# Perceiver block on one core: first transfers issued in turn with a fixed first chunk, and another order around the gate and the first expert block

## The reference

```python
x = x + xattn(layernorm(x), ctx, ctx, mask)     # 16 batches x 64 queries, 1601 keys, 16 heads of 32
x = x + attn(layernorm(x))                      # self-attention of 64 tokens, q and v with a LoRA term
x = x + ffn(layernorm(x))                       # 20 experts, top 2 of a softmax gate
...
scores = jnp.where(mask == 0, NEG, scores)      # one mask for all batches
...
h = gelu(xf @ wg1 + bg1); probs = softmax(h @ wg2 + bg2)[:, :20]
top_vals, top_idx = lax.top_k(probs, 2)
y = sum over experts of g_e * (xf @ We_e + be_e)
```

## Time and profile before

| | us |
|---|---|
| median of 3 executions | 780.59 |
| lowest, highest | 780.42, 781.32 |
| the profiled execution's own time | 780.74 |
| its span in the trace | 778.9 |
| TensorE busy | 707.7 (91%) |
| VectorE busy | 409.8 (53%) |
| ScalarE busy | 360.5 (46%) |
| GpSimd busy | 283.1 (36%) |
| mean granted TensorE clock | 0.962 |

### The profile page before, as it was taken

One profiled execution on the slowest core, in us unless ns is written; L12 is line 12 of the kernel. 1 busy time (PEld: TensorE's weight loads), 2 busy tenths in 40 slices (PEclk: granted clock), 3 DMA queues, 4 the chain that ended last, 5 costly groups with the idle time before them and its releaser, 6 DMA issues.

```text
span 778.9 us, 16989 instructions
## 1 busy us (share of the span) xinstructions
PE 707.7 (91%) x6829; PEld 582.2 (75%) x6829; DVE 409.8 (53%) x937; ACT 360.5 (46%) x664; POOL 283.1 (36%) x259
## 2 busy tenths in 40 slices
PE   0899999999999999999999999999999856999970
PEld 0697888879887888788788877887778653688860
DVE  4833334454344334533553345725377547699965
ACT  1425344544454345435453343534456331499950
POOL 0004155414542354235532453522225132666530
PEclk9999999999999999999999999999999975799995
DMA  9401101211121001100110002020001682699918
GB/s 289 150 1 43 44 2 43 98 38 62 43 98 44 18 27 43 44 16 30 44 44 2 3 3 74 8 107 10 3 29 57 232 308 98 211 372 388 340 53 323
DMA packets 30779, 74.77 MB, mean 96 GB/s; under 512 B 4052, under 2 KB 5076, under 8 KB 29666
## 3 DMA queue, kind: packets, MB, share of 16 engines
q1 hardware_dynamic: 26290, 65.16, 23.7%
q0 software_dynamic: 4400, 8.41, 3.1%
HBM read 66.13 MB, written 13.44 MB: 102 GB/s over the span
## 4 chain that ended last, share of the span: by engine, by line
PE 84%; DVE 6%; issue 4%; DMA 2%; ACT 2%; POOL 0%; SPq 0%; POOLq 0%; DVEq 0%; ACTq 0%
PE bank L187 22%; PE bank L189 20%; PE bank L188 20%; PE bank L193 11%; PE bank L346 4%; PE bank L323 3%; DVE x_sb L1602 1%; DMA xi<-scratch_xn,tok 1%; DMA wr<-scratch_ys 1%; PE bank L561 1%; PE bank L548 1%; PE bank L577 1%; DVE wh L1076 1%; DVE stats L1330 0%; ACT wh L754 0%
## 5 line engine op out<-in xcount | busy, mean ns | idle before, releaser
L1628 POOL TENSOR_SCALAR pp<-pp,rl 128x400 f32<-128x400 f32 x128 | 163.8, 1297 | 234.8 <-DVE rl L1173 234.8
L1228 DVE COPY pt<-bank 128x512 f32<-128x512 f32 x64 | 44.3, 692 | 99.4 <-PE bank L193 99.3
L187 PE MATMUL bank<-chi,wk 128*128 128x400 f32 x256 | 93.5, 365 | 0.0
L837 ACT ACTIVATE pp<-pp,acc 128x400 f32<-128x400 f32 x128 | 79.0, 619 | 28.0 <-DVE acc L1261 27.7
L1261 DVE CUSTOM_DVE_ANT_0 pp<-bank,cap 128x400 f32<-128x400 f32 x128 | 66.8, 569 | 46.5 <-PE bank L323 46.5
L189 PE MATMUL bank<-chi,wk 128*128 128x400 f32 x256 | 88.3, 345 | 0.0
L188 PE MATMUL bank<-clo,wk 128*128 128x400 f32 x256 | 88.3, 345 | 0.0
L187 PE MATMUL bank<-wv,chi 128*128 128x512 f32 x200 | 83.5, 417 | 0.0
L189 PE MATMUL bank<-wv,clo 128*128 128x512 f32 x200 | 78.5, 392 | 0.0
L188 PE MATMUL bank<-wv,chi 128*128 128x512 f32 x200 | 78.5, 392 | 0.0
L754 ACT ACTIVATE pt<-bank 128x512 f32<-128x512 f32 x64 | 38.2, 597 | 76.4 <-PE bank L193 75.3
(11 more groups left out here) (236 smaller groups left out, 1388.4 us busy)
## 6 DMA issues: line engine op xcount, KB each, us to landing
wr<-in_We SPq DMA_DIRECT2D x13, 1024.0 KB, 12.3
craw<-in_ctx SPq DMA_DIRECT2D x16, 800.0 KB, 4.3
raw<-in_We SPq DMA_DIRECT2D x8, 1024.0 KB, 9.1
acc<-in_We SPq DMA_DIRECT2D x6, 1024.0 KB, 9.6
scratch_xn<-acc SPq DMA_DIRECT2D x16, 256.0 KB
wr<-scratch_ys SPq DMA_DIRECT2D x8, 512.0 KB, 7.9
x_sb<-in_x SPq DMA_DIRECT2D x2, 1024.0 KB, 11.5
out_dram<-x_sb SPq DMA_DIRECT2D x8, 256.0 KB, 5.2
```

The lines of the kernel that those rows point to most:

```text
L187: pe.matmul(o, lhs[0], rhs[0], start=start, stop=False)
L837: act.activation(frame(p8), frame(p8), ACT.Exp, bias=bias, scale=-1.0, accum_out=total).then_inc(S["a_exp"], 1)
L1228: dve.tensor_copy(pt[:, p8 % 4, :, :].rearrange("p a c -> p (a c)"), at("t", 8 * (n - 1) + p8)[:, :]).then_inc(S["v_pt"], 1)
L1628: pool.tensor_scalar(frame(p8), frame(p8), rl[:, n % 2, p8:p8 + 1], None, ALU.mult).then_inc(S["g_pn"], 1)
```

## The change

It has two parts. In the first, the chunks are laid out in reverse in memory, so that the last 400 keys are chunk 0, and chunk 0 is always the first to be done; its context and mask are loaded without waiting for `ids`, which only decide on further chunks. The flags come from a second copy of the mask (`rows`), laid out in rows of 8,000 bytes. SP issues constants, lora, x, rows; waits for the constants and issues wq; waits for x and issues the context; waits for the mask and issues wk and the second half of x. VectorE takes all four statistics of x ahead of the mask, and works out `ids` behind the low half of wk (`used`); the small transposes and products for it are moved in TensorE's order too.

In the second, a Gelu on one column is run in step 9, Gelu of the first gate half stands in step 12 ahead of the copy of tile 7, the gate product of the first half is one pass of 512 columns, that of the second half is cut in two of 256 columns of which the first stands behind the turn of tile 6. The splits of expert weight 1 are moved, the high half behind the second Gelu, the low half into block 0 with that of weight 2. All biases stand ahead of the first turn of tokens. Weights 6 and 7 wait for gather 1 too, and go out ahead of weight 9.

```diff
@@ tensor
-            pe.wait_ge(S["v_ids"], 2)
-            pe.matmul(pb[7][0:1, 0:10], fr[:, :], cst[0:NC_, 128:138], start=True, stop=True).then_inc(S["p_ids"], 1)
...
-            for i in range(4):
-                turn_x(i)
+            turn_x(0)
+            turn_x(1)
+            pe.wait_ge(S["v_ids"], 2)
+            pe.matmul(pb[7][0:1, 0:10], fr[:, :], cst[0:NC_, 128:138], start=True, stop=True).then_inc(S["p_ids"], 1)
+            turn_x(2)
+            turn_x(3)
...
+                elif what == "ga":
+                    pe.wait_ge(S["v_n2"], 14)
+                    pe.wait_ge(*before("g1", 1))
+                    gate_part(1, slice(0, 256))
                 else:
-                    pe.wait_ge(S["v_g1"], 1)
-                    pe.wait_ge(S["v_n2"], 8 + 4 * i + 3)
-                    pe.wait_ge(*before("g1", i))
-                    for c in (slice(0, 384), slice(384, 512)):
...
+                    pe.wait_ge(S["v_n2"], 12 + 4 * i)
+                    if i == 0:
+                        pe.wait_ge(S["v_g1"], 1)
+                        pe.wait_ge(*before("g1", 0))
+                    gate_part(i, slice(256 * i, 512)).then_inc(S["p_g1"], 1)
+
+            def gate_part(i, c):
+                for k in range(4):
+                    last = mm3(pe, pb[bank_of("g1", i)][:, c], [w[:, k, :] for w in g1],
+                               [v[:, k, i * 512 + c.start:i * 512 + c.stop] for v in xu], k == 0, k == 3)
+                return last
...
-            biases(range(3, 6))
+            biases(range(3, 8))
             turn_tokens(0)
-            biases(range(6, 8))
@@ beside
-                  ([("pj", 6)], [], [("n2", 5)]), ([("pj", 7)], [], [("g1", 0), ("n2", 6)]),
+                  ([("pj", 6)], [], [("n2", 5)]), ([("pj", 7)], [], [("g1", 0), ("n2", 6), ("ga", 1)]),
@@ scalar
                 if step >= 8:
                     norms(step)
+                if step == 9:
+                    act.activation(warm[:, :], gw[:, 20:21], ACT.Gelu)
+                if step == 12:
+                    gelu(0)
...
-                if step == 11:
-                    we_hi(1)
-                if step == 12:
-                    gelu(0)
             gelu(1)
+            we_hi(1)
@@ vector
-            dve.wait_ge(S["d_cap"], 32)
...
+            def used():
...
+            dve.memset(fl[:, 0:1], 1.0)
+            dve.wait_ge(d_x[0], 16)
+            for i in range(4):
+                own.on(bn(i))
             variance(0, 4)
+
+            dve.wait_ge(S["d_cap"], 32)
+            dve.tensor_reduce(cm[:, :], mska, AX.X, ALU.max, apply_absolute_value=True).then_inc(S["v_cap"], 1)
...
+            dve.tensor_scalar(fl[:, 1:NC_], cm[:, 1:NC_], rows[:, 2:3], None, ALU.max).then_inc(S["v_ids"], 1)
             scaled(0, 4)
             apply_x(0)
             apply_x(1)
             weight_lo(wh[0], raw[:, 0], 1)
+            dve.wait_ge(S["p_ids"], 1)
+            dve.tensor_reduce(fr[:, :], pb[7][0:NC_, 0:128], AX.X, ALU.max).then_inc(S["v_ids"], 1)
             for i in range(4):
                 turn_x(i)
                 if i < 2:
                     apply_x(i + 2)
+                elif i == 2:
+                    dve.wait_ge(S["p_ids"], 2)
+                    dve.tensor_copy(frow[:, 0:10], pb[7][0:1, 0:10]).then_inc(S["v_ids"], 1)
             context(0)
             weight_lo(wk, raw[:, 1], 2)
+            dve.wait_ge(S["v_ids"], 3)
+            used()
             dve.wait_ge(d_x[1], 16)
...
-            we_lo(1)
-
...
-            biases(range(6))
+            biases(range(8))
...
             def block_of(n):
                 turn_tokens(n + 1)
+                if n == 0:
+                    we_lo(1)
+                    we_lo(2)
...
             turn_tokens(0)
-            biases(range(6, 8))
-            we_lo(2)
@@ sync
             sp.dma_start(cst[:, :], t["cst"]).then_inc(S["d_cst"], 16)
-            for h in range(2):
-                sp.dma_start(mska[64 * h:64 * h + 64, :, :], t["mask"].rearrange("c q k -> q c k")).then_inc(S["d_cap"], 16)
+            sp.dma_start(lora[:, :, :], t["lora"]).then_inc(S["d_par"], 16)
             xv = t["x"].rearrange("(i b) q d -> i (b q) d", b=2)
             sp.dma_start(x_sb[:, 0:4, :], xv[0:4].rearrange("i p d -> p i d")).then_inc(d_x[0], 16)
+            for h in range(2):
+                sp.dma_start(mska[64 * h:64 * h + 64, :, :], t["rows"]).then_inc(S["d_cap"], 16)
+            sp.wait_ge(S["d_cst"], 16)
             sp.dma_start(raw[:, 0], t["wq"]).then_inc(d_raw[0], 16)
+            sp.wait_ge(d_x[0], 16)
+            sp.dma_start(craw[:, :, :], t["ctx"][0, 0]).then_inc(S["d_ctx"], 16)
+            sp.wait_ge(S["d_cap"], 32)
+            sp.dma_start(raw[:, 1], t["wk"]).then_inc(d_raw[1], 16)
             sp.dma_start(x_sb[:, 4:8, :], xv[4:8].rearrange("i p d -> p i d")).then_inc(d_x[1], 16)
-            sp.dma_start(raw[:, 1], t["wk"]).then_inc(d_raw[1], 16)
-            sp.dma_start(lora[:, :, :], t["lora"]).then_inc(S["d_par"], 16)
...
-            chunk = chunk_of(0)
-            context(0, 0, chunk)
-            load_cap(chunk, 0)
+            for h in range(2):
+                sp.dma_start(mski[64 * h:64 * h + 64], t["mask"][0]).then_inc(S["d_cap"], 16)
+            sp.dma_start(excl[:, :], t["excl"][0]).then_inc(S["d_cap"], 16)
             sp.wait_ge(S["v_w"], 1)
             sp.dma_start(raw[:, 0], t["wv"]).then_inc(d_raw[0], 16)
...
                 elif n < R:
                     sp.wait_ge(S["p_tab"], 1)
+                    sp.wait_ge(d_xi[1], 16)
...
-            for n in (R, R + 1, 6, 7, R + 2):
+            for n in (R, 6, 7, R + 1, R + 2):
                 load_weight(n)
@@ arrays
-        "ctx": ctx.reshape(16, NC, CW, 4, 128).transpose(0, 1, 4, 3, 2),
-        "mask": mask.reshape(64, NC, CW).transpose(1, 0, 2),
+        "ctx": ctx.reshape(16, NC, CW, 4, 128)[:, ::-1].transpose(0, 1, 4, 3, 2),
+        "mask": mask.reshape(64, NC, CW)[:, ::-1].transpose(1, 0, 2),
+        "rows": mask.reshape(64, NC, CW)[:, ::-1],
```

More of the change, by code:

```diff
@@ L126, in perceiver @@
         gmg = sb("gmg", [128, 2, 8])
+        warm = sb("warm", [128, 1])
         rb = sb("rb", [128, 2, 16])
@@ L714, in perceiver @@
         place = [(("wl", k), 4 + k) for k in range(4)] + [(use, n % 3) for n, use in enumerate(ring)]
-        dense_uses = [use for step in beside for part in step for use in part if use[0] != "n2"]
+        dense_uses = [use for step in beside for part in step for use in part if use[0] not in ("n2", "ga")]
         place += [(use, n % 2) for n, use in enumerate(dense_uses)]
@@ L1101, in vector @@
[L1101 to L1116, removed]
-                dve.wait_ge(own.sem, own.n)
-                own.on(dve.scalar_tensor_tensor(out=frow[:, 15:20], in0=frow[:, 5:10], scalar=float(j + 1),
-                                                in1=frow[:, 10:15], op0=ALU.is_equal, op1=ALU.mult,
-                                                accum_out=frow[:, 20 + j:21 + j]))
@@ L1121, in vector @@
-            dve.wait_ge(own.sem, own.n)
-            dve.tensor_copy(ids[:, 0:5], frow[:, 20:25]).then_inc(S["v_ids"], 1)
-            dve.tensor_copy(ids[:, 5:6], frow[:, 9:10]).then_inc(S["v_ids"], 1)
+            def used():
+                own.on(dve.tensor_tensor(frow[:, 10:15], frow[:, 0:5], cst[0:1, 142:147], ALU.mult))
+                for j in range(NC_):
+                    dve.wait_ge(own.sem, own.n)
+                    own.on(dve.scalar_tensor_tensor(out=frow[:, 15:20], in0=frow[:, 5:10], scalar=float(j + 1),
+                                                    in1=frow[:, 10:15], op0=ALU.is_equal, op1=ALU.mult,
+                                                    accum_out=frow[:, 20 + j:21 + j]))
+                dve.wait_ge(own.sem, own.n)
+                dve.tensor_copy(ids[:, 0:5], frow[:, 20:25]).then_inc(S["v_ids"], 1)
+                dve.tensor_copy(ids[:, 5:6], frow[:, 9:10]).then_inc(S["v_ids"], 1)
@@ L1272, in cross @@
                     share(n, 3, seg)
-            own.on(bn(2))
-            own.on(bn(3))
+            dve.memset(fl[:, 0:1], 1.0)
+            dve.wait_ge(d_x[0], 16)
+            for i in range(4):
+                own.on(bn(i))
             variance(0, 4)
+            dve.wait_ge(S["d_cap"], 32)
+            dve.tensor_reduce(cm[:, :], mska, AX.X, ALU.max, apply_absolute_value=True).then_inc(S["v_cap"], 1)
+            dve.wait_ge(S["v_cap"], 1)
+            own.on(dve.tensor_scalar(cm[:, :], cm[:, :], 0.0, None, ALU.not_equal))
+            dve.wait_ge(own.sem, own.n)
+            own.on(dve.tensor_reduce(rows[:, 0:1], cm[:, :], AX.X, ALU.max))
+            dve.wait_ge(own.sem, own.n)
+            dve.tensor_scalar(rows[:, 1:2], rows[:, 0:1], SCALE, None, ALU.mult)
+            own.on(dve.tensor_scalar(rows[:, 2:3], rows[:, 0:1], -1.0, 1.0, ALU.mult, ALU.add))
+            dve.wait_ge(own.sem, own.n)
+            dve.tensor_scalar(fl[:, 1:NC_], cm[:, 1:NC_], rows[:, 2:3], None, ALU.max).then_inc(S["v_ids"], 1)
```

(4 more changed lines are left out.)

27 lines of the change are left out of this document (8 added, 19 removed).

## The result

The changed kernel takes 773.37 us (median of four runs, 771.37 to 774.41) beside 780.96 for the kernel before on the same chip: ratio 0.9904, 95% interval 0.9885 to 0.9922. A second set of five runs gave 773.86 and 0.9912 [0.9898, 0.9926]. So it is faster, by about 1%, clear of the noise: 7.6 us where 11.1 were forecast. The profiled execution took 774.41 us, span 772.6, mean granted clock 0.960 (before 0.962).

What follows compares the result with a forecast made beforehand. TensorE was taken as the bound, so only the start and the holes between projection and first expert block could shrink: 780.74 - 5.3 - 2.5 - 3.3 = 769.6 us, range 766.6 to 773.4.

Steps and rivals of the forecast that it cites:

- Part 1: Start of the kernel: earlier x and reordered issues bring the first query matmul 5.3 us earlier, bounds 2.4 to 5.7.
- x at 6.6: Start: the first half of x, issued at about 1.7, lands 4.9 us later, at 6.6 us; high bound 9.65.
- 8,000-byte rows ... if it lands like x ... at 9.3: Start: the mask, in 8,000-byte instead of 1,600-byte rows, lands about 2.7 us behind x, at 9.3.
- wq follows at 12.0: Start: wq lands at 12.0 behind the mask; landing at 14.67 as before would leave 3.2 us of the gain.
- first statistic after 9: Start: sign that would show the forecast wrong; the first statistics of x were expected near 6.6 us.
- x shares the engines: Rival, start: wq, rows and x in flight together, x near 8.6 to 9.6, gain 2.4 to 3.2, total 772.1; chance 0.17.
- short rows: Start: argument against the shared-engines rival, that the mask's 1 MB needed to 9.65 before because its rows were short.
- Part 2: Gate: warm-up Gelu, split gate product and moved weight copy bring the second Gelu 2.5 us earlier, bounds 0.5 to 4.4.
- (b): Gate: moving ScalarE's weight 1 copy and splitting the gate product put the second Gelu at 632.0, not 634.87.
- (a): Gate: the warm-up Gelu's table load at step 9 widens the hole ahead of tile 5 from 2.4 to 3.9, +1.5 us.
- Part 3: First expert blocks: biases, not gather 0, bind; first turn 5.1, block 0 7.7 behind the gather, not 11.0; 3.3 earlier.
- 3.9 us of backlog: Expert blocks: delayed weight loads leave 1.5 MB behind, cutting the last weight's lead from 4.7 to 0.7; price 0, at most 2.

Runs made afterwards that it cites:

- wq_first: Changed kernel with wq issued ahead of the two mask row transfers; one execution, 774.32 us beside 782.62 for the kernel before.
- start_only: Kernel before with only the start of the change (issues, rows, order of VectorE's first steps); 779.33 us against 781.25, ratio 0.9976.
- gate_only: Kernel before with only the gate and first-block changes, its start unchanged; 775.89 us, ratio 0.9934 to the kernel before.
- bias_banks: Changed kernel with the gate and expert bias products in a ring of five banks instead of three; 772.35 us, ratio 0.9893 to the kernel before.
- rows128: Changed kernel with mask rows laid out for 128 partitions and loaded in one transfer instead of two to 64; one execution, 773.33 us.
- mask_fifth: Changed kernel with one of five mask chunks loaded for the flags and reduced, 0.2 MB instead of 1.0; one execution, 767.68 us.

## Why the prediction was partly wrong

**Part 1 failed:** it gave 2.7 us at the first query matmul instead of 5.3, and this alone moves the 769.6 of the forecast to 772.2. The step was "x at 6.6", with "8,000-byte rows ... if it lands like x ... at 9.3" and "wq follows at 12.0". Measured: 9.0, 12.7 and 15.2. The prediction had named a first statistic after 9 as a sign that it was wrong; it came at 9.01. The reason given, that the order of landing is the order of issue, is true (wq_first), but order is not speed. Of the 2.4 us by which x was late 0.8 is x alone (5.7, where the 4.9 of wv was taken over) and 1.6 the company; and the rows, though their lines were five times longer, moved at 224 to 230 GB/s and held wq as well. The working behind the landings was right: with the rows at 12.73 put into it the scaling stands 3.1 us earlier and the first query matmul 2.7, as measured, and with one transfer to 128 partitions that matmul comes at 22.7.

The rival "x shares the engines" had the size (2.4 to 3.2 us; 2.7 measured at the first matmul), and gave 772.1. Its mechanism is half of it: beside wq x was hardly later than alone, beside the rows it was. It rested on the mask before, which had needed to 9.65, and the prediction put that aside as "short rows"; the 211 to 221 GB/s of before, at a share of 1.06 to 1.07, were there to be read, and rows five times longer did not raise them.

**A term was missing:** the clock outside the gate. The pause at 482 costs 1.3 us when the clock falls behind it, and whether it falls changes from kernel to kernel with shifts of what comes ahead. It was put at nothing, and so was the slow stretch behind the first query matmul, which happened to be 6 matmuls shorter in after's profiled run: 1.1 us in the forecast's favour, by luck, since start_only, with the same start, had 13 slow ones. The prediction looked for slow clocks only where the rows of before showed one, in the gate.

**Part 2 was right in every event** (hole 3.9, no load beside the Gelu, no second load, 21.7 to the gather), and its size depends on the clock: (b) was costed with 4.6 us from the turn of tile 5 to the end of the projection, as in before (4.66) and in gate_only (4.59); in the profiled run it took 5.95, with 0.43 a matmul throughout. From turn 5 to the second Gelu 3.0 us were saved in the profiled run, and 4.4 in gate_only; less the 1.5 of (a), that is 1.5 and 2.9, where 2.9 had been worked out and 2.5 taken (13.2 us from turn to Gelu had been worked out, 13.21 were measured in gate_only). The Trainium skill (ScalarE: Activation LUTs, What ACT_TABLE_LOAD costs) adds a drain of 1.38 us to each switch; the load began 0.02 us behind the norm, took 1.28, and its activation began 0.02 behind it, so the trace does not agree. The same page (Table sets: the hidden batching unit) says that copy and identity are in every set, and there the trace agrees: between 610 and 630.67 copies, identities and two Gelus ran without a load.

**Part 3 was right** in its cause and its two distances, 5.1 and 7.7, and bias_banks confirms that the biases bind. Of the 3.3 us 2.2 are left at token tile 3, because block 0 and the turn behind it ran at 1.2 GHz to the end (5.25 us for 12 matmuls and 1.05 for the turn). The lead of the weights never showed: landings of 15.7 at worst, 4.1 us of lead at the last weight, the same 81.24 us, so the 3.9 us of backlog were a pessimistic sum.

In the profiled runs 6.3 us stand for the 11.1 forecast. The 4.8 are: 2.6 at the first query matmul, less 1.3 that came back up to 487 (1.1 of it the fewer slow matmuls behind the first query matmul), 1.3 at the pause of 482, 1.0 in the gate, 1.1 at block 0, and 0.1 behind the last scatter. The medians, 7.6 apart, hold less of the clock's share: the other three runs beside it were 1.0 to 3.0 us faster than the profiled one. In which place they saved it no trace shows.

## What to carry to other kernels

When transfers are reordered, take for each a landing time of its own form and its own company: here it moved landings by 1.4 to 2.7 us whether the rows went in two transfers to 64 partitions or in one to 128, and longer rows did nothing for the rate of the mask. A DMA share of 1.0 says nothing without the GB/s beside it. Cost a stretch behind a pause of TensorE at both clock levels, with the measured rows of each, and where only waiting would stand there, matmuls that nobody reads can be worth more than they cost. Compare two profiles from point to point before calling an effect absent: in rows128 it was there to the last scatter. A step placed "in idle time" belongs ahead of the wait, not behind it.

## What the runs showed of the hardware

1 MB to 2 x 64 partitions moved at 224 to 230 GB/s with the engines' share at 1.0 to 1.05, the same 1 MB to 128 partitions, from rows laid out twice in memory, at 422 to 434. A pause of TensorE of 0.7 us was followed, in six kernels of twelve, by about 3.4 us at 1.2 GHz, 1.3 us of loss; filled with matmuls, in the two kernels tried, by none, which proves little beside six unfilled ones without a fall. Behind the 3.9 us hole filled, the turn took 0.66 and all went at 2.4 GHz; unfilled, the turn took 1.1 us in after (0.66 in wq_first and mask_fifth) and part or all of the projection went at 1.2. And TensorE at work is not always enough: from 644 to 666, busy for 87% of it, up to 660 with bias products of 20 partitions, the table product and turns, the granted clock stayed at 0.50, well into block 0.
